# Vision tower with eight experts on one core: VectorE's order of work inside one tile of the expert stage

## What is computed

```python
h = tok(x)                        # 64 images of 2x104x104: shifts, norm, 8x8 patches -> 169 tokens of 128
h = concat([cls_tok, h])          # 170 tokens an image, 10,880 rows of 128
h = h + gated_linear_attention(layernorm(h))
h = h + ffn(layernorm(h))

def ffn(x):                       # per token the best 2 of 8 experts
    gate_vals, idx = top_k(x @ router_w, 2)
    gates = softmax(gate_vals)
    for e in range(8):
        t = relu(x @ w1[e] + b1[e]) @ w2[e] + b2[e]
        y = layernorm(x + t) * gamma[e] + beta[e]
        out = out + gate_of_e * y
```

## Time and profile before

| | |
|---|---|
| median of 3 runs | 921.68 us (920.68 to 923.33) |
| the profiled execution | 921.47 us, its span 919.7 us |
| mean granted TensorE clock | 0.943 of full speed |
| busy: TensorE, VectorE, ScalarE, GpSimd | 801.1 (87%), 743.3 (81%), 571.0 (62%), 504.0 (55%) us |
| expert stage | about 560 to 884 us of the span |

### The profile page before, as it was taken

The page is one execution under the profiler, slowest core; times in us unless marked ns, Lnnn a source line. Parts: engine busy times, 40 slices in busy tenths (PEclk is TensorE's granted clock), DMA queues, the critical chain, the costliest instruction groups (busy, mean ns, idle before and its releaser), DMA issues.

```text
span 919.7 us, 27974 instructions
## 1 busy us (share of the span) xinstructions
PE 801.1 (87%) x7821; PEld 684.4 (74%) x7822; DVE 743.3 (81%) x3194; ACT 571.0 (62%) x1536; POOL 504.0 (55%) x660
## 2 busy tenths in 40 slices
PE   1799999888999999999999638999999999999910
PEld 1699999875677777777777526999999999999910
DVE  2768777833789999989999752999999999999987
ACT  2633344015889999999999523666676666676610
POOL 3000000000078888888788782778877777877850
PEclk9999999998999999999999558999999999999965
DMA  8544330034011212122121226422222222222489
GB/s 181 124 80 82 61 62 1 1 115 144 23 55 54 60 57 62 54 60 60 51 63 55 63 86 206 164 80 76 79 73 76 74 74 73 80 74 76 125 299 376
DMA packets 68637, 84.19 MB, mean 92 GB/s; under 512 B 12118, under 2 KB 52745, under 8 KB 68157
## 3 DMA queue, kind: packets, MB, share of 16 engines
q1 hardware_dynamic: 52727, 53.27, 21.4%
q0 software_dynamic: 12256, 22.50, 7.9%
q10 hardware_dynamic: 3555, 7.23, 2.3%
HBM read 48.15 MB, written 35.71 MB: 91 GB/s over the span
## 4 chain that ended last, share of the span: by engine, by line
PE 47%; DVE 28%; issue 10%; ACT 4%; DMA 3%; SPq 2%; DVEq 2%; ACTq 1%; POOL 1%; POOLq 0%
PE ps L697 9%; DVE arena L1400 7%; PE ps L797 5%; DVE arena L1066 4%; PE ps L772 4%; DVE arena L1421 3%; PE ps L783 3%; PE ps L846 3%; PE ps L832 3%; PE ps L851 3%; PE ps L778 2%; DVE arena L1383 2%; PE ps L865 2%; PE ps L956 2%; PE ps L761 2%
## 5 line engine op out<-in xcount | busy, mean ns | idle before, releaser
L578 POOL DMA_INDIRECT x_slots<-arena x192 | 191.9, 1000 | 58.1 <-POOL arena L576 45.7
L607 POOL DMA_INDIRECT y_tokens<-arena x184 | 187.4, 1018 | 46.1 <-issue 45.2
L956 PE MATMUL ps<-arena 128*128 x1472 | 180.5, 276 | 0.2 <-ACT arena L1663 0.2
L956 PEld LDWEIGHTS ps<-arena 128*128 128x128 f32 x1472 | 171.6, 192 | 1.6 <-issue 0.3
L1663 ACT ACTIVATE arena<-ps,b_t 128x256 f32<-128x256 f32 x368 | 144.6, 475 | 29.1 <-PE ps L947 19.8
L697 PE MATMUL ps<-wt,arena 128*128 128x128 f32 x960 | 123.9, 289 | 12.0 <-DVE arena L1066 12.0
L697 PEld LDWEIGHTS ps<-wt,arena 128*128 128x128 f32 x960 | 118.5, 203 | 13.4 <-DVE arena L1066 13.4
L583 POOL MEMSET arena<- 128x258 f32 x1 | 0.3, 319 | 193.6 <-DVE arena L1317 193.6
L945 PE MATMUL ps<-arena 128*128 128x256 f16 x368 | 101.3, 275 | 5.1 <-DVE arena L1369 5.1
L946 PE MATMUL ps<-arena 128*128 128x256 f16 x368 | 101.2, 275 | 0.0
L947 PE MATMUL ps<-arena 128*128 128x256 f16 x368 | 101.1, 275 | 0.0
(11 more groups left out here) (216 smaller groups left out, 1785.2 us busy)
## 6 DMA issues: line engine op xcount, KB each, us to landing
arena<-x_slots SPq DMA_DIRECT2D x92, 130.0 KB
h<-h_rows SPq DMA_DIRECT2D x1, 5440.0 KB
arena<-y_tokens SPq DMA_DIRECT2D x17, 320.0 KB
out<-h ACTq DMA_DIRECT2D x17, 320.0 KB, 3.5
arena<-x_in SPq DMA_DIRECT2D x64, 84.5 KB
arena<-x_in SPq DMA_DIRECT2D x56, 78.0 KB
h_rows<-h SPq DMA_DIRECT2D x32, 128.0 KB
arena<-y_tokens SPq DMA_DIRECT2D x1, 3200.0 KB, 14.8
```

The source lines that it names most:

```text
L578: pool.indirect_dma_start(xs_dram, bass.IndirectOffsetOnAxis(ap=slot_i[n][0:rows, t, k:k + 1], axis=0), row[n][0:rows, k, t, :], None).the ...
L607: pool.indirect_dma_start(y_dram, bass.IndirectOffsetOnAxis(ap=y_id[n % YBUF][:, k:k + 1], axis=0), y_sl[n % YBUF][:, k, :], None, bounds_ ...
L956: ins = pe.matmul(ps[6 + m][:, 128 * k:128 * k + 128], hid[m][:, c, 128 * k:128 * k + 128], w2_sb[:, bass.ds(e, 1), c, :].rearrange("p o n ...
```

## The change

VectorE does the younger tile's statistics (lag 3) directly behind the lower half, before the older tile's normalisation (lag 4), and the younger tile's aggregations before the older tile's scaling. Everything else stays.

```diff
             def tile_iteration(at):
                 at(0, lower_half)
+                at(3, tile_stats)
                 at(4, tile_norm)
-                at(3, tile_stats)
+                at(3, tile_moments)
                 at(4, scaled)
-                at(3, tile_moments)
                 at(4, shifted)
                 at(2, sums)
                 at(3, gated_rstd)
```

## The result

The changed kernel took 924.25 us (median of 22 runs, 919.55 to 930.87), the kernel before 920.82 us (22 runs). The ratio is 1.0047, 95% interval 1.003 to 1.0064: slower by about half a per cent (3.4 us between the medians, 4.3 us by the ratio). I had forecast 920.8 us and no change that can be told.

What follows compares the result with a forecast made beforehand. VectorE was taken to bound a loop pass, GpSimd right behind. Seven tiles at -0.04, first tile +0.44 and turn -0.26 made -0.10 us a pass, -0.9 over nine passes: 920.8 us, range 916.5 to 927.

Steps and rivals of the forecast that it cites:

- the tile's term: Expert loop, tiles behind a pass's first: 0.06 us shorter by VectorE's sequence, taken as -0.04 because GpSimd can hold VectorE back.
- What bounds: Expert loop: VectorE's own sequence sets the 27.60 us pass, with GpSimd right behind it in between.
- rival D: Expert loop: GpSimd's 3.23 us alone paces a tile, only first tile and turn change; no effect, 923.3 us, chance 0.08.
- The statistics cost nothing beside L599: Tile's start, T to T + 0.40: VectorE's statistics run beside GpSimd's addition unblocked, charged nothing.
- Rival C: Statistics blocked by GpSimd's addition, +0.5 us in 63 tiles, +28 us on top of the gain forgone: 949 us, chance 0.03.
- The aggregation starts at T + 1.15: T is the start of the first instruction behind the lower half; aggregation follows the normalisations' end by 0.15 us.
- CAST at T + 1.79: CAST waits for the scaling's end, 0.45 us after its start; T starts the first instruction behind the lower half.
- CAST to the next T: Tile's end, CAST to the first instruction behind the next lower half: unchanged at 1.36 us.
- First tile +0.44: First tile of a pass: no GpSimd addition beside it, pays 0.40 us of exposed ends plus 0.04 for registers.
- Turn -0.26: Turn of the loop: the earlier aggregation lets ScalarE finish, so L1394 starts 0.33 us behind the sum instead of 0.59.
- The sixteen tiles ahead of the loop and the tail: Sixteen tiles: TensorE bound, covered; tail: two tiles lose 0.4 us each, hidden by GpSimd, 0.8 without that cover.
- Rival B: Wait behind the normalisations dearer than 0.15 us; 0.10 more a tile gives 928 us, 0.05 gives 924.4; chance 0.27.

Runs made afterwards that it cites:

- experiment 1: Kernel before with only the statistics moved ahead of the normalisations, aggregations left behind the scaling: 925.74 us, ratio 1.0067.
- experiment 6: Changed kernel with two buffers for mean and variance and without GpSimd's addition of the second bias: 908.08 us, ratio 0.9901 to the kernel before.
- experiment 7: Changed kernel with two buffers for mean and variance, and CAST issued before VectorE's wait for the scaling: 918.02 us, ratio 0.9992 to the kernel before.
- experiment 3: Kernel before without GpSimd's addition of the second bias: 912.3 us, ratio 0.9909.
- experiment 4: Changed kernel without GpSimd's addition of the second bias: 920.49 us, ratio 1.0015 to the kernel before.
- experiment 5: Kernel before with only the aggregations moved ahead of the scaling, behind the statistics: 950.55 us (four runs), ratio 1.0355.
- controls of 8 and 11: Kernel before, old order, with two buffers for mean and variance, run twice: ratio 0.9999 on a chip with lower TensorE clock, then 921.99 us, 1.0028.
- experiment 2: Changed kernel with two buffers for mean and variance, so the aggregation need not wait for the normalisation ahead: 916.9 us, ratio 0.9972 to the kernel before.

## Why the prediction was wrong

The places in the loop were right, the sizes of two terms were not, and they did not cancel. What failed is the tile's term: put at -0.04 us, it measured +0.08.

- *What bounds.* Right for the turn and the first tile behind it, which VectorE sets. Wrong for the tiles in between in the kernel before, where GpSimd was not "right behind". Experiments 1, 6 and 7 show GpSimd's row as a floor of 3.23 to 3.28 us under the tiles that VectorE does faster, as soon as it has caught up behind a turn. In the kernel before it was so already: VectorE alone needs 2.74 (experiment 3), and the 3.23 that I read as VectorE's sequence was GpSimd's. The rival D had this floor, at 0.08.
- *The statistics cost nothing beside L599.* Right: 0.28 us each. Rival C is out.
- *The freed ports give back 0.48.* Right: the pair fell from 1.07 to 0.59.
- *The aggregation starts at T + 1.15.* Measured T + 1.12 (725.45 to 726.57). *L1410 at T + 1.34*: 1.37. *CAST at T + 1.79*: 1.83.
- *CAST to the next T, "which the change leaves as it is", 1.36.* It is 728.67 - 727.28 = 1.39 (728.34 and 0.33): L1421 starts 0.12 behind CAST instead of 0.09, and in the trace the computation of its address now starts behind CAST and no longer ahead of it. With this 0.03 and the 0.04 up to CAST a free tile is 3.22, not 3.15. The larger slip up to CAST is from L1389 to L1410, 726.82 - 726.57 = 0.25 where I had 0.19: L1410 starts only at L1390's end. The aggregation's own early start gives 0.03 of it back.
- *"0.06 less than now ... I take 0.04".* This is the term that turned the sign. Six tiles went from 19.31 to 19.82 us, +0.085 each, where I had -0.04. 0.07 of the difference is the free tile above. The six tiles' excess of 0.5 us over 3.22 each is half meetings with GpSimd (19.82 against 19.57), and half two delays of VectorE's queue that experiment 4 has too (its tiles of 3.34 and 3.33): L1410 0.10 late in one tile, as in the one shown, and CAST 0.10 late in the next. I had priced meetings only at L1400. Over seven tiles it was -0.28 and measured +0.53 (0.51 and 0.02), so the term is off by 0.8 us a pass.
- *First tile +0.44.* Measured +0.49. Right but for 0.05.
- *Turn -0.26.* Measured -0.63. L1394 starts 720.13 - 719.79 = 0.34 behind the sum, as said. But L1394 to L1369 also shrank, from 1.99 to 1.61, and that I did not foresee. That the early aggregation does it is shown by experiments 1 and 5, and how by the branch and the load of VectorE's sequencer (duration in ns, then the start), before and changed:

```profile
L392 DVEq COMPARE_BRANCH  x1: 56/56/56, 722.5 to 722.5; - x1
L379 DVEq TENSOR_LOAD <-expert_tab x1: 1224/1224/1224, 723.0 to 723.0; - x1
...
L392 DVEq COMPARE_BRANCH  x1: 56/56/56, 719.9 to 719.9; - x1
L379 DVEq TENSOR_LOAD <-expert_tab x1: 1143/1143/1143, 720.4 to 720.4; - x1
```

Before, the branch passes at 722.5, behind the L1394 that waits for ScalarE and 0.7 us behind the sum's start (721.86). In the changed kernel nothing holds L1394, and the branch passes at 719.9, 0.1 behind the sum's start (719.79) and ahead of L1394 itself; the load is 0.08 shorter besides. In experiment 1 it passes 0.6 behind the sum's start, with L1394 late again, in experiment 5 0.2 ahead of it.

- *The sixteen tiles ahead of the loop and the tail, nothing, or 0.8 us.* The tail was not hidden: 28.0 us against 26.5, 1.5 more. The first sixteen took 56.1 and 57.0 us in the two traces of the changed kernel against 53.8 to 55.1 in three of the old order (the kernel before and the controls of 8 and 11). For the tail I had read one row of GpSimd's as cover, for the first sixteen no row at all. Why they grew no run here isolates; the new order with two buffers has 53.8 to 55.8 in its three traces.

Sum: I had -0.10 a pass, measured +0.40. Rival B had the sign and a wait dearer by 0.05 to 0.10 a tile; the time came out at its edge, though it was not the wait behind the normalisation that was dearer (0.14, I had 0.15) but many small things after it. Rival C's sum was off, too: 63 tiles of 0.5 are 31.5 us, not 28.

By the Trainium skill (page "VectorE: DVE Perf Modes", section "The DRAIN you can't avoid") the waits would have cost nothing. Experiment 2 contradicts it here: taking one wait away shortens a first tile by 0.24 us.

## What to carry to other kernels

An instruction that is blocked by another engine is not idle room that a reorder wins: if the other engine's own row is as long as the tile, the block only moves. Before moving work that stands between a producer and its consumer on one engine, add up what each lost cover exposes; here a wait for the instruction in front cost 0.24 us with the overlap, and a second buffer for a few words took it away again. Look at the turn of a loop by itself: here it answered to a mean and variance that came 0.6 us earlier, with more than any tile did.

## What the runs showed of the hardware

- Batch norm statistics and aggregations of VectorE run beside GpSimd's addition undisturbed (0.28 and 0.17 us), while the normalisation (1.07 instead of 0.59 a pair) and a CAST (0.49 instead of 0.13, rows 8) are held until it ends.
- A wait of VectorE for its own last instruction starts the next one 0.04 us behind its end when the waiting instruction carries the wait itself, 0.14 to 0.16 when a semaphore increment or a register computation lies between (CAST 0.04 in the tile at 725.11, 0.16 in experiment 2's first tile).
- VectorE's sequencer passes a loop's branch while instructions ahead of it still run, unless a wait holds one of them: 0.1 us behind the start of the sum in the changed kernel, 0.7 in the kernel before, where L1394 in front of it waited for ScalarE.
